# Attention on one core: scores and bias head by head, and the first head pair of a batch going up the blocks of queries

## The reference, cut to what matters

```python
# bias of a head is a function of the distance i - j only
h = silu(ln(pos @ w0 + b0, g0)); h = silu(ln(h @ w1 + b1, g1)); bias = (h @ w2 + b2)[i - j]
xn = ln(x, g_norm)
q  = l2norm(xn @ Wq) * q_scale               # 16 heads
k, v = split(xn @ Wkv)                       # one key head, one value head
k = l2norm(concat(null_k, k)) * k_scale;  v = concat(null_v, v)
sim  = q @ k.T * 8 + bias                    # causal
attn = softmax(sim);  out = ln((attn @ v) @ Wout, g_out)
x + ternary_linear(round_to_int8(out))       # rows quantised by their largest entry
```

## Time and profile before

| | us |
|---|---|
| median of 3 runs | 1564.64 (1559.87 to 1564.86) |
| the profiled execution | 1564.24 |
| its span, first to last instruction | 1562.5 |

### The profile page before, as it was taken

How to read it: one execution, slowest core, us unless ns; L and a number is a source line. 1 busy time by engine, 2 the same in 40 slices (tenths; PEclk the granted TensorE clock), 3 DMA queues, 4 the chain that set the end, 5 groups by cost and what they waited for, 6 DMA issues and landing times.

```text
span 1562.5 us, 39526 instructions
## 1 busy us (share of the span) xinstructions
PE 1434.3 (92%) x13844; PEld 935.6 (60%) x13844; DVE 1199.8 (77%) x2071; ACT 1041.8 (67%) x2140; POOL 1262.5 (81%) x908
## 2 busy tenths in 40 slices
PE   4888995999999999997997995999999999997996
PEld 2444552777777777774443552777777777776442
DVE  4455885788788788784997885788888888886797
ACT  4664654889888888886112563788888888888110
POOL 4564755999999999997653663999999999999553
PEclk9999996999999999998999997999999999999998
DMA  7003874111211201201885885111111121110796
GB/s 213 1 1 72 176 146 84 44 27 42 47 24 42 48 23 42 51 6 30 173 189 142 159 164 105 41 42 42 29 42 42 29 42 42 29 29 5 143 192 148
DMA packets 225620, 114.93 MB, mean 74 GB/s; under 512 B 193200, under 2 KB 193712, under 8 KB 225456
## 3 DMA queue, kind: packets, MB, share of 16 engines
q1 hardware_dynamic: 220864, 104.42, 31.9%
q10 hardware_dynamic: 4608, 8.39, 1.5%
HBM read 58.11 MB, written 8.54 MB: 43 GB/s over the span
## 4 chain that ended last, share of the span: by engine, by line
PE 58%; POOL 11%; issue 9%; DVE 7%; DMA 3%; ACT 2%; SPq 1%; DVEq 0%; POOLq 0%; ACTq 0%
PE ps L1322 15%; PE ps L1286 12%; PE ps L1289 11%; PE ps L1255 10%; POOL work L577 7%; PE ps L1361 4%; PE ps L1308 4%; DVE work L1058 4%; POOL work L590 2%; DMA work<-work 1%; DMA tab<-bias_table 1%; POOL work L607 1%; SPq L452 1%; DVE work L1077 1%; PE ps L1370 1%
## 5 line engine op out<-in xcount | busy, mean ns | idle before, releaser
L577 POOL TENSOR_TENSOR work<-work 128x1024 f16<-128x1024 f32 (+3 forms) x592 | 932.6, 1624 | 28.5 <-ACT work L749 28.5
L1058 DVE SCALAR_TENSOR_TENSOR work<-ps,tab 128x1024 f32<-128x1024 f32 (+3 forms) x640 | 668.5, 1057 | 171.6 <-PE ps L1289 140.1
L749 ACT ACTIVATE work<-work 128x1024 f32<-128x1024 f32 (+3 forms) x640 | 572.9, 922 | 157.5 <-DVE work L1058 152.9
L1322 PEld LDWEIGHTS ps<-vals,work 128*128 128x128 bf16 (+1 forms) x7936 | 435.4, 99 | 108.6 <-POOL work L577 6.7
L1322 PE MATMUL ps<-vals,work 128*128 128x129 f16 (+1 forms) x7936 | 460.8, 207 | 4.0 <-POOL work L577 3.1
L1286 PE MATMUL ps<-qo,kT 128*128 128x512 f16 (+3 forms) x1280 | 345.5, 352 | 30.3 <-DVE work L1058 15.9
L1289 PE MATMUL ps<-qo,kT 128*128 128x512 f16 (+3 forms) x1280 | 344.6, 351 | 0.0
L1289 PEld LDWEIGHTS ps<-qo,kT 128*128 128x128 f16 x1280 | 123.4, 99 | 119.3 <-issue 6.3
L1361 PE MATMUL ps<-wout,work 128*128 128x512 f16 x768 | 174.0, 385 | 18.2 <-DMA work<-work 18.2
L1255 PE MATMUL ps<-wq,tab 128*128 128x512 f16 x768 | 177.3, 381 | 0.4
L1361 PEld LDWEIGHTS ps<-wout,work 128*128 128x128 f16 x768 | 75.9, 99 | 111.7 <-DMA work<-work 18.4
(11 more groups left out here) (135 smaller groups left out, 1276.3 us busy)
## 6 DMA issues: line engine op xcount, KB each, us to landing
tab<-bias_table SPq DMA_DIRECT2D x64, 512.0 KB, 4.6
tab<-in_x SPq DMA_DIRECT2D x64, 256.0 KB, 3.1
out_x<-work ACTq DMA_DIRECT2D x32, 256.0 KB, 2.3
work<-in_L_cond_Wq SPq DMA_DIRECT2D x1, 2048.0 KB, 8.7
work<-in_L_cond_Wout SPq DMA_DIRECT2D x2, 1024.0 KB, 10.2
qo<-in_L_cond_w SPq DMA_DIRECT2D x1, 1024.0 KB, 7.3
work<-work SPq DMA_TRANSPOSE x64, 4.3
qo<-in_L_cond_b SPq DMA_DIRECT2D x2, 256.0 KB, 5.4
```

The costliest lines, as they stand in the source:

```text
L577: pool.tensor_tensor(low[:, k % LRING, :, c0:512], probs[:, r, :, c0:512], high[:, r, :, c0:512], ALU.subtract).then_inc(low_pool, 1)
L749: act.activation(probs[:, k % RING, :, c0:512], probs[:, k % RING, :, c0:512], ACT.Exp).then_inc(expd, 1)
L1058: dve.scalar_tensor_tensor(out=probs[:, k % RING, :, c0:512], in0=ps[:, 2 * (k % 2):2 * (k % 2) + 2, c0:512], scalar=SCORE, in1=tab[:, :, ...
L1322: last = pe.matmul(ps[:, sum_bank(i, q), (t % SUMS) * VS:(t % SUMS) * VS + w], parts[:, rings[part], e, s * P:(s + 1) * P], vals[:, j, 0:w ...
```

## The change

Two things are done.

**Head by head.** `score` does both halves of head 0, then both of head 1. Each head has its own `scored` and `biased` semaphore, `bias` is two instructions of one head each, and the next unit but one may write a head's bank as soon as that head's bias is done. ScalarE still takes one exp per unit, when both are done.

**Up the blocks.** The first head pair of a batch (`UP`) goes through the blocks 0, 1, 2, 3, the others (`DOWN`) as before. TensorE's waits at the start of `attend` become `ready`: block i asks only for its own queries and keys, and unit 0 and 1 for the bank that the projection used. The turn of the last key tile is left out of the last projection step and done behind unit 1. The probability ring begins at slot 4 (`FIRST`). SyncE loads the first two table pieces inside the projection's steps (`first_tables`), the other two behind it.

```diff
+class Order:
+    def __init__(self, blocks, first_null):
+        self.units = [(i, j) for i in self.blocks for j in range(4 * i + 4)]
+        self.nulls = {at((i, 4 * i + 1)): i for i in self.blocks[1:]}
+        self.nulls[first_null] = self.blocks[0]
...
+UP = Order(range(NB), 6)
+DOWN = Order(reversed(range(NB)), 4 * NB - 3)
...
+                def first_table(i):                                   # SyncE
+                    sp.wait_ge(tab_ld, 16 * (b * HP * NB + i) + 16)
+                    sp.dma_start(tab[:, :, 512 * i:512 * i + 512], ...).then_inc(tab_ld, 16)
+
+                def first_tables(t, u):
+                    if t != NT - 1:
+                        return
+                    sp.wait_ge(table_stored, 16)
+                    for u in range(2):
+                        sp.wait_ge(b_xd[u], 16 * (NT // 2) * (b + 1))
+                    sp.wait_ge(c_xb, NT * b + 2)
+                    first_table(0)
+                    first_table(1)
...
-                return [(load_x, 0), (turn_q, 6), (turn_x, 1)], attend, ...
+                return [(load_x, 0), (turn_q, 6), (turn_x, 1), (first_tables, 3)], attend, ...
...
                 def attend():                                         # GpSimd
                     pool.wait_ge(b_pn, b + 1)
-                    with pool.Fori(0, HP) as hp:
-                        for k in POOL_LOW:
-                            low_part(hp, k)
+                    pool.wait_ge(b_lo, NT * (b + 1))
+                    for k in UP.pool_low:
+                        low_part(0, UP, k)
+                    with pool.Fori(1, HP) as hp:
+                        for k in DOWN.pool_low:
+                            low_part(hp, DOWN, k)
...
-                    act.wait_ge(biased, n + 1 + CB)                   # ScalarE, exps
+                    for e in range(2):
+                        act.wait_ge(biased[e], n + 1 + CB)
...
+                    if order is UP and turn == 0:                     # ScalarE, null_part
+                        act.wait_ge(b_pn, b + 1)
+                        for u in range(2):
+                            act.wait_ge(b_qd[u], 16 * (NT // 2) * (b + 1))
...
+                    if order is UP and j == 0:                        # VectorE, bias
+                        dve.wait_ge(tab_ld, 16 * (before + i + 1) + 16)
...
-                    dve.wait_ge(scored, n + 1)
                     dve.wait_ge(pv_done, n + 1)
-                    dve.scalar_tensor_tensor(out=probs[:, k % RING, :, c0:512],
-                                             in0=ps[:, 2 * (k % 2):2 * (k % 2) + 2, c0:512], scalar=SCORE,
-                                             in1=tab[:, :, x0:x0 + 512 - c0], ...).then_inc(biased, 1)
+                    for e in range(2):
+                        dve.wait_ge(scored[e], n + 1)
+                        dve.scalar_tensor_tensor(out=probs[:, (FIRST + k) % RING, e, c0:512],
+                                                 in0=ps[:, 2 * (k % 2) + e, c0:512], scalar=SCORE,
+                                                 in1=tab[:, e, x0:x0 + 512 - c0], ...).then_inc(biased[e], 1)
...
+                def ready(k):                                         # TensorE
+                    i, j, c0 = UP.unit(k)
+                    if k < 2:
+                        pe.wait_ge(b_qn, NT * (b + 1) + 1 + k)
+                    if j == 0:
+                        pe.wait_ge(b_cd, NT * b + 4 * i + 4 + 1)
+                        pe.wait_ge(b_vl, NT * b + 4 * i + 4 + 1)
+                        for u in range(2):
+                            pe.wait_ge(b_qd[u], 16 * (NT // 2 * b + 2 * i + 2))
...
-                    pe.wait_ge(biased, n - 1 + CB)
+                    if order is UP:
+                        ready(k)
                     for e in range(2):
-                        pe.matmul(..., kT[:, 0, ...], ..., start=True, stop=False)
-                    for e in range(2):
-                        last = pe.matmul(..., kT[:, 1, ...], ..., start=False, stop=True)
-                    last.then_inc(scored, 1)
+                        pe.wait_ge(biased[e], n - 1 + CB)
+                        for half in range(2):
+                            last = pe.matmul(..., kT[:, half, ...], ..., start=half == 0, stop=half == 1)
+                        last.then_inc(scored[e], 1)
...
                     for hp in range(HP):                              # TensorE, attend
+                        order, behind = ((UP, None), (DOWN, UP), (DOWN, DOWN))[min(hp, 2)]
                         for k in range(NU):
-                            score(hp, k)
-                            weigh_slot(hp, k)
+                            score(hp, order, k)
+                            if hp == 0 and k == 1:
+                                b_turn_k(NT - 1, (NT - 1) % 2)
+                            weigh_slot(hp, order, behind, k)
```

More of the change, by code:

```diff
@@ L62 @@
 HP = H // 2
-BLOCKS = tuple(reversed(range(NB)))
-UNITS = [(i, j) for i in BLOCKS for j in range(4 * i + 4)]
-NU = len(UNITS)
+NU = sum(4 * i + 4 for i in range(NB))
 RING = 10
@@ L74 @@
 LAG = 6
+FIRST = 4
 JOIN = 15
@@ L85 @@
 WHOLE_KEYS = (3,)
-WHOLE = tuple(k for k, (i, j) in enumerate(UNITS) if j in WHOLE_KEYS and j < 4 * i)
-POOL_LOW = tuple(k for k in range(NU) if k not in WHOLE)
 SUMS = 3
@@ L93, with unit, turn, bank @@
 LATE = (0, 2, 3)
-NULLS = {UNITS.index((i, 4 * i + 1)): i for i in BLOCKS}
-DRAINS = {}
-for i, q in itertools.product(BLOCKS, range(3)):
-    DRAINS[max([UNITS.index((i, 4 * i + 1 + q)) + LAG + LATE[q] + 1] + [slot + 1 for slot in DRAINS])] = (i, q)
-STORES = {UNITS.index((i, 4 * i + 3)) + LAG + LATE[2] + 2: i for i in BLOCKS}
-def unit(k):
-    i, j = UNITS[k]
-    return i, j, P * max(0, j - 4 * i)
-def turn(i):
-    return NB - 1 - i
-def sum_bank(i, q):
-    return 4 + (SUMS * turn(i) + q) % 4
+class Order:
+    def __init__(self, blocks, first_null):
+        self.blocks = tuple(blocks)
+        self.units = [(i, j) for i in self.blocks for j in range(4 * i + 4)]
+        at = self.units.index
+        self.whole = tuple(k for k, (i, j) in enumerate(self.units) if j in WHOLE_KEYS and j < 4 * i)
+        self.pool_low = tuple(k for k in range(NU) if k not in self.whole)
+        self.nulls = {at((i, 4 * i + 1)): i for i in self.blocks[1:]}
+        self.nulls[first_null] = self.blocks[0]
+        self.drains = {}
+        for i, q in itertools.product(self.blocks, range(3)):
+            self.drains[max([at((i, 4 * i + 1 + q)) + LAG + LATE[q] + 1] + [slot + 1 for slot in self.drains])] = (i, q)
+        self.stores = {at((i, 4 * i + 3)) + LAG + LATE[2] + 2: i for i in self.blocks}
+    def unit(self, k):
+        i, j = self.units[k]
+        return i, j, P * max(0, j - 4 * i)
+    def turn(self, i):
+        return self.blocks.index(i)
+    def bank(self, i, q):
+        return 4 + (SUMS * self.turn(i) + q) % 4
+UP = Order(range(NB), 6)
+DOWN = Order(reversed(range(NB)), 4 * NB - 3)
 def since(eng, semaphore, count):
@@ L437, in attend @@
+                    first_table(3)
+                    for i in DOWN.blocks:
+                        table_piece(1, i, UP.units.index((NB - 1, 4 * (NB - 1 - i) + 3)))
+                    with sp.Fori(2, HP) as hp:
+                        for i in DOWN.blocks:
+                            table_piece(hp, i, DOWN.units.index((i, 4 * i + 3)))
                     sp.wait_ge(expd, (b + 1) * HP * NU)
@@ L1076, in drain, with heads @@
                     dve.wait_ge(o_added, 3 * m + q + 4)
[L1077 removed]
+                    dve.tensor_tensor(part, acc[:, :, 0:VW], null_tmp[:, turn % 2, t0:t0 + n, :], ALU.add).then_inc(o_part_in, 1)
                     dve.wait_ge(o_part_in, 3 * m + q + 1)
[L1079 removed]
+                    dve.tensor_tensor(o_sum[:, turn % 2, t0:t0 + n, :], acc[:, :, VW:VS], part[:, :, 0:DH], ALU.add
                                       ).then_inc(o_added, 1)
                     if q == 2:
[L1082 to L1084 removed]
+                        dve.reciprocal(rec[:, turn % 2, :], o_part[:, :, DH]).then_inc(o_rec, 1)
+                def heads(hp, order, behind):
                     for k in range(NU):
[L1086 to L1090 removed]
+                        if k in order.drains:
+                            drain(hp, order, *order.drains[k])
+                        if behind and k + NU in behind.drains:
+                            drain(hp - 1, behind, *behind.drains[k + NU])
+                        bias(hp, order, k)
                 def attend():
@@ L1099, in attend @@
                         dve.wait_ge(c_out[u], 16 * (NT // 2) * b + 16)
-                    heads(0, True)
-                    with dve.Fori(1, HP) as hp:
-                        heads(hp, False)
-                    for k in sorted(DRAINS):
+                    heads(0, UP, None)
+                    heads(1, DOWN, UP)
+                    with dve.Fori(2, HP) as hp:
+                        heads(hp, DOWN, DOWN)
+                    for k in sorted(DOWN.drains):
```

(4 more changed lines are left out.)

165 lines of the change are left out of this document (81 added, 84 removed).

## The result

The changed kernel took 1536.32 us (median of 4 runs, 1534.34 to 1537.19), before 1563.18 us (4 runs). The ratio is 0.9828, 95% interval 0.9815 to 0.984: 26.9 us saved. Forecast were 1542 us, range 1537 to 1557, and 22.6 us saved.

A forecast was written before the change was run, and what follows sets the result against it. GpSimd was taken as the bound, with 28.5 us idle before its low parts; 8.3 + 8.1 us of earlier starts and 2 x 3.1 us of gaps made 22.6 us, from 1564.24 to 1542 us, range 1537 to 1557.

The forecast's parts named there:

- GpSimd is the bound, and only its start can be gained: Attention: each stage lasts as long as GpSimd's 296 low parts; only its idle time, 28.5 us in all, can be saved.
- The start, 8.3 and 8.1 us: Start of each batch's attention: GpSimd's first low part comes 8.3 us earlier in batch 0, 8.1 in batch 1.
- the walk: First units followed through the engines from key turn 14 at 238.38 us to GpSimd's first low part at 245.4.
- The gaps, 3.1 us a batch of 3.9: Behind GpSimd's first low parts: 0.8 us idle, at unit 8, instead of 3.9, saving 3.1 us a batch.
- Rival 2: Batch start: TensorE's clock stays at its lower level to the first weighing, 9 us back, 1551; chance 0.12.
- Head by head costs nothing and saves nothing: Steady attention: VectorE's extra instructions, up to 6.3 us a pair, stay hidden behind GpSimd; costed at zero, saving nothing.
- Rivals 1 and 3: VectorE's second instruction stalls TensorE: by a quarter, 14 us back, 1556, chance 0.11; by half, 1581, chance 0.06.
- The tables: Batch start: table pieces 0 and 1, asked for early, land at about 231.5 and 236.5 us, no longer late.
- the cover of 3 us: SyncE's queue: the transpose behind the early table pieces goes some 1 us later, hidden with 3 us to spare.

The follow-up runs named there:

- again: The changed kernel run once more with no edit, beside before: 1537.27 us, ratio 0.9833 to before.
- up_only: The changed kernel with head by head undone (one bias instruction for both heads, one pair of semaphores), up the blocks kept: 1539.15 us, ratio 0.9846 to before.
- tables_late: The changed kernel with all four table pieces asked for behind the last transpose of q, as before: 1561.55 us, ratio 0.9986 to before.

## Why the prediction was right, and where it was not

- **GpSimd is the bound, and only its start can be gained.** The first half is right, for the kernel as it was; the second is the step that failed (see head by head, below). The cut kernel before shows how thin the first was: with a sixth of GpSimd's work gone, a pair still took 58.04 us, 0.23 less. TensorE with its waits for VectorE was the second bound, hardly behind; the "0.7 us a pair" read from its busy time was not the slack.
- **The start, 8.3 and 8.1 us.** Measured 8.29 and 8.06 against the last q low part, though this whole stretch ran 2.56 us sooner. From key turn 14 to the first low part the walk gave 245.4 - 238.4 = 7.0 us, the trace 242.84 - 235.82 = 7.02. The terms hold one by one: key turn done by 239.6, copy, table load, exp, low part.
- **The gaps, 3.1 us a batch of 3.9.** Mis-sized: no gap was left, and the low parts of a batch took 4.0 and 4.1 us less (470.2 and 470.3 to 466.2). I put units 4 to 6 at 1.6 to 1.7 us of TensorE's time each, the lower level of its clock throughout. In the trace the twelve matmuls of units 4 to 6 go from 240.72 to 243.31, 0.22 us each, the upper level. Before, TensorE was at the lower level until 262.24, and had stood for 6.19, 1.10 and 2.77 us ahead of its units 0, 2 and 3; in the changed kernel it had no stand over 0.2 us between the key turn at 235.82 and 240.72, and the clock had risen by then. ScalarE began its null part 247.01 - 235.82 = 11.2 us behind the key turn, where the prediction had 251.3 - 238.4 = 12.9. So unit 8 was in time, and the start and the gaps together gave 24.4 us where the sum had 22.6: 1.8 of the 4.3 us missed. Rival 2 (the clock stays low) was wrong in sign.
- **Head by head costs nothing and saves nothing.** In attention this holds within what can be told (942.3 against 942.5 us, again against up_only). The failed step is the sentence behind it, that nothing outside GpSimd's idle time can be saved: it put at nothing what moving the code can do, and one semaphore more moved VectorE's code and took 2.5 us out of the first stage (241.1 to 238.6), the larger part of the 4.3 us. Chance has a part in how far out the time lies. The range's lower end was the idle time alone, taken from a median of 1564.64 us; before's median over four runs is 1563.18, and 26.9 us off the first is 1537.7, inside the range. Without the 2.5 us of the first stage the time would be 1538.8, inside it as well.
- **Rivals 1 and 3 (VectorE's second instruction lands on TensorE).** Refuted, and the other way round: with GpSimd out of the way head by head makes a pair 0.88 us shorter, 58.04 to 57.16. VectorE's second instruction cost 0.05 us, not 0.157, and TensorE had the banks back earlier. The Trainium skill ("VectorE: DVE Perf Modes", section "The TRN2 errata") names a fixed cost of 120 cycles per instruction out of PSUM, 125 ns as an estimate at its 0.96 GHz; the single rows agree in kind (0.157 us for one more), and instructions that follow each other without a wait don't (0.05 to 0.06).
- **The tables.** Pieces 0 and 1 were asked for at 224.4 and 229.6 us, and the cover of 3 us held. tables_late shows that without this part, which I priced in one paragraph, the whole gain in attention is gone.

## What to carry to other kernels

Find the engine that is never idle in the steady stretch, and walk only its first instruction back; all waits that end together there must go together, since leaving one in gives most or all of the gain back. Price the second bound by taking the first away, not by busy time: it may be 0.2 us behind with 0.7 us idle. Moving work from one of two bounds that lie so close to the other gains nothing. And before a few us are given to a mechanism, look at the stages that the change doesn't touch: here one entry in an instruction stream was worth 2.4 us.

## What the runs showed of the hardware

- TensorE's granted clock fell behind a stand of 1.97 us and not behind one of 1.54 us in the same code (0.81 and 1.00 over 53 to 62 us).
- VectorE's bias of 128x512 took 0.68 us alone and 0.62 us in a row of four, one of 128x1024 1.22 and 1.18.
- A VectorE subtraction of 128x1024 with both inputs in SBUF, beside GpSimd's, which do the same, took 1.29 to 2.13 us in nine of 16 and 5.26 to 5.58 us in seven; all seven ended 1.1 us behind the moment at which GpSimd ran out of work. The Trainium skill, "SBUF — State Buffer", section "Who interferes with whom", says that a VectorE instruction with two SBUF inputs contends with a GpSimd instruction that reads SBUF. The trace agrees, and adds that the wait can be longer than two of GpSimd's instructions (1.9 us each).
- VectorE's bias, with one input in PSUM, came in twice as many instructions at no loss to GpSimd: 932.6 and 932.4 us for its 592 low parts.
